# A new instruction order for the second chunk of the first expert mixture, and five-tile score rows moved one key tile into their banks

## The reference

```
x = x + attn0(ln(x))   # 16 heads of width 8, no mask, its own scale and bias
x = x + ffn0(ln(x))    # 8 experts of 64 hidden units, best 2, and a shared expert
x = x + attn1(ln(x))   # 8 query heads, 4 key heads of width 128, rotary, causal
x = x + ffn1(ln(x))    # 16 experts, best 4, clipped gated units
```

```
scores = sigmoid(x @ gate_W) * route_scale        # x here is ln(x)
topk_scores, topk_idx = top_k(scores, 2)
topk_w = topk_scores / topk_scores.sum(-1)
gate_full = topk_w spread over the 8 experts
h = gelu(x @ W1 + b1);  y = h @ W2 + b2           # per expert
out = sum_e gate_full[e] * y[e] + (gelu(x @ Ws1 + bs1) @ Ws2 + bs2)
```

## Time and profile before

| | us |
|---|---|
| median of 3 runs (982.52 to 983.34) | 982.95 |
| profiled execution, its own time | 979.61 |
| its span, first to last instruction | 977.5 |
| PE busy | 900.5 (92%) |
| VectorE busy | 729.1 (75%) |
| ScalarE busy | 620.4 (63%) |
| GpSimd busy | 360.5 (37%) |

### The profile page before, as it was taken

The page is one execution under the profiler, slowest core; times in us unless marked ns, Lnnn a source line. Parts: engine busy times, 40 slices in busy tenths (PEclk is TensorE's granted clock), DMA queues, the critical chain, the costliest instruction groups (busy, mean ns, idle before and its releaser), DMA issues.

```text
span 977.5 us, 17521 instructions
## 1 busy us (share of the span) xinstructions
PE 900.5 (92%) x6208; PEld 583.6 (60%) x6208; DVE 729.1 (75%) x1499; ACT 620.4 (63%) x1251; POOL 360.5 (37%) x401
## 2 busy tenths in 40 slices
PE   3689999999999999979699999999999999898998
PEld 1312223222222322535588889888988899787897
DVE  7789999999999998648655554655455547797877
ACT  3268888888888888534755555555555554365665
POOL 5700000000000010221676769396929683246422
PEclk9779999999999999989899999999999999999999
DMA  2410111110000000000000000000000012000000
GB/s 67 140 51 24 42 42 39 45 44 19 25 22 18 18 2 18 1 0 18 1 1 1 1 17 1 2 11 7 1 1 2 1 34 55 1 2 12 11 13 12
DMA packets 23374, 20.10 MB, mean 21 GB/s; under 512 B 5176, under 2 KB 17440, under 8 KB 23288
## 3 DMA queue, kind: packets, MB, share of 16 engines
q1 hardware_dynamic: 23288, 18.99, 6.6%
HBM read 14.26 MB, written 4.59 MB: 19 GB/s over the span
## 4 chain that ended last, share of the span: by engine, by line
PE 62%; DVE 20%; POOL 8%; issue 4%; ACT 2%; DMA 2%; SPq 1%; DVEq 0%; POOLq 0%; ACTq 0%
DVE halves L831 13%; PE a_sum L2182 8%; PE summed L1045 7%; PE m_down L2438 6%; PE score_bank L1032 5%; PE a_turn L2167 4%; PE max_bank L992 4%; PE max_bank L1005 3%; PE a_scores L1700 3%; PE a_scores L1701 3%; PE a_scores L1702 3%; POOL a_crossed L1780 2%; POOL a_rotated L1782 2%; PE m_hid L2256 1%; PE m_hid L2257 1%
## 5 line engine op out<-in xcount | busy, mean ns | idle before, releaser
L956 ACT ACTIVATE probs<-score_bank 128x512 f32<-128x512 f32 x512 | 267.6, 602 | 74.7 <-PE score_bank L1032 74.5
L831 DVE TENSOR_REDUCE halves<-max_bank 128x2 f32<-128x1024 f32 x256 | 298.6, 1219 | 11.8 <-PE max_bank L992 9.7
L1715 ACT ACTIVATE a_probs<-a_scores,a_lowest 128x896 f32<-128x896 f32 (+7 forms) x128 | 94.8, 741 | 113.7 <-DVE a_lowest L1710 112.9
L2182 PE MATMUL a_sum<-a_v,a_turned 128*128 128x128 f32 x1152 | 164.6, 280 | 2.4 <-ACT a_turned L2042 1.5
L2182 PEld LDWEIGHTS a_sum<-a_v,a_turned 128*128 128x128 f32 x1152 | 145.0, 193 | 3.5 <-ACT a_turned L2042 2.1
L992 PE MATMUL max_bank<-k_stack,q_stack 48*128 48x512 bf16 x512 | 117.9, 398 | 25.2 <-DVE halves L831 24.3
L1045 PE MATMUL summed<-probs,v_tile 128*32 128x512 f32 x1024 | 138.7, 614 | 0.0
L1032 PE MATMUL score_bank<-q_stack,k_stack 50*128 50x512 bf16 x512 | 132.5, 385 | 3.6 <-ACT probs L956 2.2
L1710 DVE TENSOR_REDUCE a_lowest<-a_scores 128x1 f32<-128x896 f32 (+7 forms) x128 | 96.2, 755 | 34.1 <-PE a_scores L1704 32.8
L754 POOL COPY v_tile<-values 128x128 f32<-128x128 f32 x16 | 4.6, 293 | 303.9 <-PE summed L1045 303.7
L992 PEld LDWEIGHTS max_bank<-k_stack,q_stack 48*128 48x128 bf16 x512 | 25.3, 94 | 124.0 <-DVE halves L831 109.9
(11 more groups left out here) (343 smaller groups left out, 1630.7 us busy)
## 6 DMA issues: line engine op xcount, KB each, us to landing
rope<-in_rope SPq DMA_DIRECT2D x8, 256.0 KB, 3.1
rope<-in_L_ffn_mlp_w SPq DMA_DIRECT2D x8, 256.0 KB, 4.8
q_parts<-l_q_parts SPq DMA_DIRECT2D x2, 768.0 KB, 4.9
k_parts<-l_k_parts SPq DMA_DIRECT2D x2, 768.0 KB, 6.4
q_stack<-q_parts SPq DMA_DIRECT2D x30, 48.0 KB
k_stack<-k_parts SPq DMA_DIRECT2D x30, 48.0 KB
x<-in_L_attn_x SPq DMA_DIRECT2D x2, 512.0 KB, 4.2
q_stack<-shift SPq DMA_DIRECT2D x64, 2.0 KB
```

Of the source, the lines that this page charges most:

```text
L831: dve.reduce_max(halves[:, u % 2, half, :].rearrange("p (x t) -> p x t", x=2)[:, :, qt], max_bank[place % RING][:, :, :], AX_X).then_inc(f ...
L956: act.activation(probs[:, step % PROBS, x, :], score_bank[e % SCORES][:, :], ACT.Exp, scale=SCALE0).then_inc(prob_ready, 1)
L1715: act.activation(probs[:, k % 2, c, 0:row_width(n)], scores[n % 2][:, 0:row_width(n)], ACT.Exp, bias=lowest[:, n % 8:n % 8 + 1], accum_out ...
L2182: last_use = pe.matmul(sum_bank[:, c * P:(c + 1) * P], turned[:, m % SLOTS, i * P:(i + 1) * P], v[:, b, first + i, q, :], start=(first + i ...
```

## The change

It has two parts. In the mixture, PE's order for chunks 0 and 1 is written out in full: `up(2, 0)` leaves the end of chunk 0, `gate(0)` takes its place behind the second `turn_in`, `gate(1)` follows the shared matmul of chunk 1, and the units of chunk 2 stand behind the later expert pairs. The gate gets a place of its own: part and gate share one bank, `routing_bank`, the parts in its first half and the gate's results in the second. GpSimd does both splits after the second conversion. VectorE weighs three hidden pairs before `m0.rank` and the fourth between `m0.rank` and `m0.mark`. ScalarE takes `m0.score` right behind the second copy of the turned input, and `leave(1)` stands two activations earlier. No instruction is added or left out.

In the attention a row of five key tiles starts 128 columns into its banks, so that its pieces have 384 and 256 columns.

```diff
-        part_bank = ps("m0_part", [3 * E0, CH], BF16)
+        routing_bank = ps("m0_routing", [P, CH])
+        part_bank, gate_bank = routing_bank[0:3 * E0, 0:CH // 2].bitcast(BF16), routing_bank[:, CH // 2:CH // 2 + TB * E0]
@@ on_vector
-            weigh_hidden(1, 0)
-            weigh_hidden(1, 1)
+            for m in range(3):
+                weigh_hidden(1, m)
             dve.wait_ge(prob_ready, 1)
             m0.rank(dve, chain, 1)
-            weigh_hidden(1, 2)
+            weigh_hidden(1, 3)
             m0.mark(dve, chain, 1)
-            weigh_hidden(1, 3)
@@ on_gpsimd, after the conversion of chunk c
-                if c < FIRST:
-                    pool.wait_ge(tr_out, c + 1)
-                    m0.raise_in(pool, FIRST + c).then_inc(tr_high, 1)
-                    pool.wait_ge(tr_high, c + 1)
-                    m0.lower_in(pool, FIRST + c).then_inc(tr_low, 1)
-                    pool.wait_ge(tr_low, c + 1)
                 if c == 1:
+                    split_turned(0)
+                    split_turned(1)
@@ on_scalar
             take_turned(FIRST + 1)
+            act.wait_ge(gate_ready, 2)
+            m0.score(act, gate_bank, 1).then_inc(prob_ready, 1)
             for j in range(3):
                 activate(act, 2, j)
-            act.wait_ge(gate_ready, 2)
-            m0.score(act, spare, 1).then_inc(prob_ready, 1)
+            leave(1)
             for j in range(3, NU):
                 activate(act, 2, j)
-            leave(1)
@@ on_tensor
+            def gate(part):
+                pe.wait_ge(tr_out, part + 1)
+                if part == 0:
+                    pe.wait_ge(partT_out, FIRST)
+                m0.gate(pe, gate_bank, 1, part).then_inc(gate_ready, 1)
...
+            sum_expert(0, 3)
+            up(pe, 1, 4)
+            turn_in(FIRST + 1)
+            gate(0)
+
+            first_weights(1)
+            sum_shared(1)
+            gate(1)
+            sum_expert(1, 0)
+            spread_weights(1, 2)
+            pe.wait_ge(done.freed, done.last_place + 1)
+            turn_sum(0)
+            sum_expert(1, 1)
+            spread_weights(1, 3)
+            up(pe, 2, 0)
+            sum_expert(1, 2)
+            up(pe, 2, 1)
+            sum_expert(1, 3)
+            for j in range(2, NU):
+                up(pe, 2, j)
+            pe.wait_ge(parts_ready, 1)
+            turn_parts(2)
+            up(pe, 3, 0)
+
+            for c in range(FIRST, NCH):
+                first_weights(c)
+                sum_shared(c)
...
@@ layer1_attention
+        def row_start(n):
+
+            return P if row_width(n) == CH + P else 0
+
+        def row_pieces(n):
+
+            width, first_piece = row_width(n), min(row_width(n), CH - row_start(n))
+            return [(0, first_piece)] + ([(first_piece, width - first_piece)] if width > first_piece else [])
+
+        def row_of(n):
+            return scores[n % 2][:, row_start(n):row_start(n) + row_width(n)]
```

More of the change, by code:

```diff
@@ L1252, in take_parts @@
                 dve.wait_ge(partT_ready, c + 1)
-                dve.tensor_copy(weightT[:, cols], part_bank[:, :]).then_inc(partT_out, 1)
+                dve.tensor_copy(weightT[:, cols], part_bank).then_inc(partT_out, 1)
             def weigh_hidden(c, m):
@@ L1321, in on_gpsimd, with split_turned @@
         def on_gpsimd(pool):
+            def split_turned(c):
+                pool.wait_ge(tr_out, c + 1)
+                m0.raise_in(pool, FIRST + c).then_inc(tr_high, 1)
+                pool.wait_ge(tr_high, c + 1)
+                m0.lower_in(pool, FIRST + c).then_inc(tr_low, 1)
+                pool.wait_ge(tr_low, c + 1)
             for c in range(NCH):
@@ L1388, in turn_parts @@
                 for k in range(4):
-                    last = pe.transpose(part_bank[:, k * P:(k + 1) * P],
-                                        m0.parts[:, 4 * c + k, :, :].rearrange("p a e -> p (a e)"), m0.identity16[:, :])
+                    last = pe.transpose(part_bank[:, k * P:(k + 1) * P], m0.parts[:, 4 * c + k, :, :].rearrange("p a e -> p (a e)"), m0.identity16[:, :])
                 last.then_inc(partT_ready, 1)
@@ L1408, in turn_next, with sum_shared, sum_expert, first_weights @@
                 transpose_tiles(pe, hid_bank[c], a1.normed, t.identity[:, :], c).then_inc(next_turned, 1)
+            def gate(part):
[3 more added lines that the diff above has]
+                m0.gate(pe, gate_bank, 1, part).then_inc(gate_ready, 1)
+            def sum_shared(c):
+                wait_from(pe, out_ready, c)
+                pe.wait_ge(act_ready, c * NU + 1)
+                pe.wait_ge(part32_ready, c + 1)
+                pe.matmul(sum_bank[:, :], m0.ws2[:, :], shared[m0.shared_rows, c % 2, :], start=True, stop=False).then_inc(shared_used, 1)
+            def sum_expert(c, m):
+                pe.wait_ge(weighed_ready, c * NP0 + (m + 1))
+                last = pe.matmul(sum_bank[:, :], m0.w2[:, m, :], weighed[:, m, :], start=False, stop=(m == NP0 - 1))
+                if m == NP0 - 1:
+                    last.then_inc(sum_ready, 1)
+            def first_weights(c):
+                pe.wait_ge(partT_out, c + 1)
+                spread_weights(c, 0)
+                spread_weights(c, 1)
             pe.wait_ge(done.mix_weighed, 1)
@@ L1413, in on_tensor @@
             up(pe, 0, 3)
[L1414 to L1424, removed]
+            first_weights(0)
+            up(pe, 0, 4)
+            up(pe, 1, 0)
+            sum_shared(0)
+            sum_expert(0, 0)
+            spread_weights(0, 2)
+            up(pe, 1, 1)
+            sum_expert(0, 1)
+            spread_weights(0, 3)
+            up(pe, 1, 2)
+            turn_parts(1)
+            sum_expert(0, 2)
+            up(pe, 1, 3)
+            turn_in(FIRST)
+            sum_expert(0, 3)
[23 more added lines that the diff above has]
+                sum_shared(c)
                 for m in range(NP0):
[L1426 to L1429, removed]
+                    sum_expert(c, m)
                     if m + 2 < NP0:
@@ L1433, in on_tensor @@
                         up(pe, c + 1, m + 1)
[L1434 to L1447, removed]
+                    if m == 0:
                         turn_sum(c - 1)
[L1449 to L1452, removed]
+                    if c == FIRST and m == 0:
                         turn_parts(3)
-                    if c + 2 < NCH and m == NP0 - 1:
-                        up(pe, c + 2, 0)
                     if c == FIRST and m == 1:
@@ L1695, in score @@
             tile = half * QB + c
[L1696 to L1699, removed]
+            width, at = (tile + 1) * P, row_start(n)
+            for first, cols in row_pieces(n):
+                dst, rows = scores[n % 2][:, at + first:at + first + cols], slice(tile * P, (tile + 1) * P)
                 pe.matmul(dst, qT[0][:, b, q, rows], kT[0][:, b, first:first + cols], start=True, stop=False)
@@ L1702, in score @@
                 pe.matmul(dst, qT[1][:, b, q, rows], kT[0][:, b, first:first + cols], start=False, stop=first + cols < width)
-            pe.matmul(scores[n % 2][:, width - P:width], identity16[:, :], mask16[:, :], start=False, stop=True).then_inc(score_ready, 1)
+            pe.matmul(scores[n % 2][:, at + width - P:at + width], identity16[:, :], mask16[:, :], start=False, stop=True).then_inc(score_ready, 1)
         def row_width(n):
             return (BLOCKS[n // QB % NB][2] * QB + n % QB + 1) * P
+        def row_start(n):
[5 more added lines that the diff above has]
+            return scores[n % 2][:, row_start(n):row_start(n) + row_width(n)]
         def find_lowest(dve, n):
-            dve.tensor_reduce(out=lowest[:, n % 8:n % 8 + 1], in_=scores[n % 2][:, 0:row_width(n)], op=ALU.max, axis=AX_X,
+            dve.tensor_reduce(out=lowest[:, n % 8:n % 8 + 1], in_=row_of(n), op=ALU.max, axis=AX_X,
                               negate=True).then_inc(lowest_ready, 1)
@@ L1714, in exponentiate @@
             k, c = divmod(n, QB)
-            act.activation(probs[:, k % 2, c, 0:row_width(n)], scores[n % 2][:, 0:row_width(n)], ACT.Exp,
+            act.activation(probs[:, k % 2, c, 0:row_width(n)], row_of(n), ACT.Exp,
                            bias=lowest[:, n % 8:n % 8 + 1], accum_out=weight[:, k % 4, c:c + 1]).then_inc(prob_ready, 1)
```

## The result

The changed kernel takes 971.18 us (median of 4 runs, 969.32 to 974.48), the one before 983.14 us: a ratio of 0.9882 with a 95% interval of 0.9855 to 0.991, so 12.0 us, and by the interval 8.8 to 14.3. Forecast were 974.3, in a range of 971.5 to 978.0. The profiled execution took 971.26 us of its own time and its span is 969.1, against 979.61 and 977.5.

A forecast was written before the change was run, and what follows sets the result against it. PE was taken to bound the kernel, full in the second attention and stopped 4.56 us in the first mixture. The mixture's order (7.2 us) and five-tile rows (1.5) off 982.95 gave 974.3 us, range 971.5 to 978.0.

The forecast's parts named there:

- What bounds the kernel: PE is full in the second attention, 30.00 of 30 us; a microsecond off its stream comes off the end.
- The PE stream of the new order: First mixture, last `turn_in` to `turn_parts(2)`: 12.60 us plus waits of 0.3 and 0.1, so 7.2 us saved.
- The table load: ScalarE, before the second chunk's gate exponential: the load runs ahead of the wait, starts at 416.3 and is hidden.
- VectorE's margin of 0.45: Second chunk: ranking takes 2.32 us, fourth multiplication done by 423.7, PE at its matmul at 424.15.
- rival 3: First mixture: VectorE's chain is late and PE stops again for about 1 us; 975.2 to 976 us, chance 0.10.
- Part two: Attention rows of five key tiles: pieces of 384 and 256 save 0.10 per row, 15 times, 1.5 us; bounds 0 to 1.9.
- Rival 1: Attention rows of five key tiles: short pieces cost only their columns, saving 0; 975.7 us, chance 0.12.
- The sum: Whole kernel: 982.95 less 8.7 (7.2 and 1.5) gives 974.3 us; bounds 973.0 to 976.7.
- Rival 2: PE's clock falls inside the mixture's new stretch, costing 1.7 to 3.4 us; 976.0 to 977.7 us, chance 0.15.
- The sign "1.00 from 400 to 464": Profile after, first mixture: PE's granted clock was to be 1.00 from 400 to 464 us.

The follow-up runs named there:

- parts_early: The changed kernel with VectorE ranking before the third hidden multiplication and `turn_parts(2)` one unit earlier on PE, ahead of `up(2, 4)`; ratio to the kernel before 0.9895.
- order_only: The changed kernel with its score rows as before, so only the mixture's new order; 974.5 us, ratio to the kernel before 0.9923.
- gate_late: The changed kernel with the second gate set moved behind the second expert pair; ratio to the kernel before 0.99.
- six_shifted: The changed kernel with rows of six key tiles shifted too, into pieces of 384 and 384; 972.18 us, ratio to the kernel before 0.9921.
- before_again: The kernel before, unchanged, measured once more; ratio 0.9994, its 12 times from 977.79 to 982.90 us.
- rank_first: The changed kernel with VectorE ranking before it weighs the third hidden pair; ratio to the kernel before 0.9886.
- short_shifted: The changed kernel with rows of one, two and three key tiles also starting one tile into their bank; 970.45 us, ratio to the kernel before 0.9897.
- units_early: The changed kernel with the third chunk's hidden units (`up`) in their old places; ratio to the kernel before 0.9925.
- rows_only: The kernel before with only the shifted rows of five key tiles, mixture as before; ratio 0.9999.
- after_again: The changed kernel, unchanged, measured a second time; ratio to the kernel before 0.9912, 8.6 us faster.
- rows_again: The kernel before with only the shifted rows of five key tiles, measured a second time; ratio 0.9996.

## Why the prediction was right, point by point

- **What bounds the kernel**: right. B is 32.1 in every trace but `parts_early`, and from the last mask to the end it is 127.7 before and after, so what A lost reached the end; `order_only` shows 7.6 of 7.6, with an interval of 5.3 to 9.9.
- **The PE stream of the new order**: 12.60 and 0.4 of waits make 13.0; measured are 12.62. The mechanism was right and the sum 0.4 too high: an expert pair followed by an `up` takes 1.62 (425.03 to 426.65), not 1.75; the waits were about the forecast's size, 0.24 before `up(2, 4)` and 0.1 before `turn_parts(2)`. The shift is 7.58, forecast 7.2.
- **The table load**: right; it started at 418.92 when the copy before it ended, 2.4 before the exponential. By the Trainium skill, page "ScalarE: Activation LUTs", section "What ACT_TABLE_LOAD costs", a switch is about 2.66 with its drain, and by that the exponential would have been held until an estimated 421.6; it began at 421.34, so the trace does not bear the drain out here either.
- **VectorE's margin of 0.45**: the weakest step. The ranking took 2.62 to the next multiplication, not 2.32. Its first instruction took 0.82 instead of 0.20, while the 0.35 of idle time that the 2.32 held did not come back; in `gate_late`, with neither, it is 2.00. PE came to its fourth pair 9.12 behind the turn, not 9.25. Of the margin 0.06 was left, so rival 3 stayed away by little. `gate_late` shows the chain just past its limit.
- **Part two**: 0.09 per row (medians 1.06 and 0.97), forecast 0.10; 1.25 in the stretch where it can be read, forecast 1.5 for all. `six_shifted` shows that only the pieces of 128 were too dear: a piece of three matmuls takes 0.28 with 128 columns, 0.36 with 256, 0.53 with 384 and 0.70 with 512, so 0.17 for each 128 columns above 256 and 0.08 below. That it is the load of the weights that holds up the short ones, as the prediction says, is not shown: no run changes the loads. Rival 1, the columns alone, falls in every trace. That the time of part two is real in the median of many executions is not shown.
- **The sum**: 7.6 and 1.3 are 8.9, the forecast 8.7. Of the 12.0 of the first measurement some 3 are neither part: the second measurement has 8.6. The range was too narrow on this side: it allowed one microsecond of spread below its bounds, while the times of one kernel run over 5 (969.32 to 974.48 for the changed kernel, 977.79 to 982.90 in `before_again`), and the first measurement has four times of each kernel. The traces show where executions of one kernel differ: by the low spell at 395 the last turn lies between 413.6 and 418.3, with no relation to the kernel, and each late low spell in C costs 1.5.
- **Rival 2**, the clock: not in the changed kernel, in none of its two traces nor in the five kernels next to it (`order_only`, `rank_first`, `gate_late`, `parts_early`, `short_shifted`); but in `units_early` and, with the old order, in `rows_only`. Its price was set at 1.7 to 3.4; the two spells cost 3.4 and 5.2. Its reason, the few columns of the gates, is not what these two traces show: both times the clock fell in the shared matmul. The sign "1.00 from 400 to 464" failed at both ends in the changed kernel: the spell at the mixture's start went on to 402.1, and the next began at 463.5.

## What to carry to other kernels

Lay the new instruction stream of the full engine end to end with start-to-start distances from the old trace, and check each engine that it waits for against it: that gave 13.0 for 12.6. A stop of the matmul engine can cost its length and a half clock behind it (here 4.56, and 3.5 us at 0.50 behind it), so count both. Shorter gains than the spread of the executions are read in a stretch whose clock is full in every trace: 1.25 of 316 is plain there, and lost in the times. Where several matmuls share a row of columns, avoid pieces of 128 columns: here three of them took 0.28, where their share of columns would be half of the 0.35 of 256.

## What the runs showed that was not expected

- **A VectorE instruction four times as long beside GpSimd.** `L241`, 64 columns of f32, takes 0.20 in the earlier trace rows and in `gate_late`, where GpSimd had finished at 420.70. In the changed kernel it began at 423.28 and ended at 424.10, just behind GpSimd's subtraction (423.06 to 424.06). `after_again`, `order_only` and `short_shifted` have the same with 0.81, 0.79 and 0.82; in `rank_first` it took 0.36, from 422.01 to 422.37, where GpSimd's split ended at 422.33. The Trainium skill, page "SBUF — State Buffer", section "Who interferes with whom", has a port pair of SBUF shared by the two engines as an exclusive lock, which a `tensor_scalar` can need; the trace agrees, 0.82 against 0.20.
- **A busy engine can lose its clock.** In `rows_only` and `units_early` the clock was 0.50 for 10.2 and 6.8 us while PE was busy all the time. A wait for GpSimd of 1.3 and 1.1 had ended 2.1 and 2.2 us before the fall. `before`, `before_again` and `rows_again` had the same wait and kept the clock, so what brings the fall is open. The same order had so an A of 25.12 in one execution and 19.97 in another.
- **The wait that looks like the second prize is none.** Filling 0.8 of the 1.4 behind GpSimd moved the end of the long stop by 0.85, but A by only 0.46, since the half clock behind the stop lasted 0.8 longer, and the time by nothing measurable.
